# A four-layer graph network in one kernel: when the feature gathers of the first phase are issued, and where attention weights lie

## The chip, the cores and the metric

The kernel runs on one core of a Trainium2 chip. The metric is the device time of one execution in microseconds (us). TensorE (PE) multiplies matrices and transposes; VectorE (DVE) does comparisons, scans and elementwise work; ScalarE (ACT) applies functions and copies; GpSimd (POOL) issues the indirect DMAs, which gather or scatter rows by a list of indices; SyncE (SP) issues plain DMAs.

## What is computed

A graph has 100000 nodes with 16 features and 50000 edges sorted by their target node. Four residual layers follow each other, each on the layer-normed and rectified features: two graph attention (GAT) layers, two relational layers, a sum over edges with a rational message, and relational attention. The attention layer is cut here to what matters:

```
h = (x @ W).reshape(N, heads, outc)
e = leaky_relu(alpha_s[src] + alpha_d[dst], 0.2)
m = segment_max(e, dst);  p = exp(e - m[dst])
z = segment_sum(p, dst);  alpha = p / (z[dst] + 1e-16)
out = segment_sum(h[src] * alpha[:, :, None], dst) + b
```

Every node has a loop to itself besides. The first attention layer has 3 heads of 32 channels, the second one head of 32.

## The kernel before

The kernel is a sequence of phases. Each allocates its own buffers and semaphores and consists of one program for each engine; between two phases stands a barrier of all engines. Nodes lie 800 to a partition (C), edges 392 to a partition (T). A helper `hold(engine, sem, value)` (L50) makes an engine wait for a semaphore. Another, `paced` (L58), lets gather number s wait until the batch of eight gathers that lies two batches back has landed.

**Phase a** (64 to 1305 us) has three parts for the engines other than POOL. First comes a histogram of the edges by target: for each of NB = 56 batches of TB = 7 edge columns VectorE writes 14 one-hot tiles in fp16 (L514, L515), and TensorE adds up 14 products of them in two PSUM banks (L600) and raises `hist_ok` at the batch's end; VectorE waits for `hist_ok` of the batch two back. Then one chain of operations on VectorE turns counts into positions. The dense part follows: the node features are normed (L412 to L426), and in NSUB = 50 sub-steps TensorE transposes (L613), scores (L620), multiplies up to four half parts of the hidden layer in four banks (L632), ScalarE takes ReLU and Exp of each half part (L674, L676), VectorE combines them (L584) and raises `act_ok` once for each half part, so 200 times, and TensorE multiplies down (L643). SyncE stores the results. POOL meanwhile issues 392 gathers of input rows into `pay` (L497), one for each edge column, in one loop with `paced` (L496) in front of each. The rows in `pay` are first used in the next phase, c, which sorts the edges and scatters them to their places, four scatters a group.

**Phase g1** (2120 to 3041 us) is the first attention layer over edges. POOL gathers 336 columns of source rows (L1091). Edges are treated in nine chunks. For a chunk VectorE computes scores and arguments into `pr`, ScalarE takes their Exp in place (L1179), and VectorE multiplies the gathered rows by the weights (L1238), copies the weights (L1241) and runs 51 scans (L1244) that sum along the edges of a target. `pr` lies in SBUF. Then the sums are normalised and mixed, and 25 sub-steps like those of phase a follow: transposes (L1114), up products in the four banks from column 1024 (L1127), ScalarE (L1193, L1195), VectorE (L1340), down products (L1138) and rows (L1315). Before the four up products of a sub-step TensorE waits for `exp_ok` of the whole previous sub-step.

**Phase g2** (3041 to 3900 us) does the same for the second attention layer with one head: gathers into a ring (L1427) that POOL fills when `ring_free` says so, Exp in place in `pr` (L1537), product, copy and 33 scans a chunk (L1577 to L1581).

All phases after g2 are the same in both kernels.

Of the kernel before, what the change touches and what calls it, by code (L numbers as in the profile page):

```python
# [5 lines left out]
ALU = mybir.AluOpType  # L6
# [7 lines left out]
P = 128  # L14
# [60 lines left out]
def gnn_kernel(nc, x, src, dst, edge_attr_16, edge_type_8, edge_type_90, edge_weight,  # L75
# [45 lines left out]
    with ExitStack() as top:  # L121
# [43 lines left out]
        with ExitStack() as ctx:  # L165
# [3 lines left out]
            def sem(name):  # L169
                return semaphore(ctx, name)  # L170
# [269 lines left out]
        with ExitStack() as ctx:  # L440
# [10 lines left out]
            COLS = Q * FEAT  # L451
            SUB = 16
            NSUB = C // SUB
            PER = Q // SUB
            hi = tmp("hi", [P, 2, TB, 2, P], F16)
            lo = tmp("lo", [P, 2, TB, LO], F16)
# [33 lines left out]
            with nc.Block() as block:  # L490
                @block.gpsimd
                def _(pool):
                    nc.gpsimd.iota(home[:], pattern=[[1, C]], base=SLOTS, channel_multiplier=ROWS,
                                   allow_small_or_imprecise_dtypes=True).then_inc(home_ok, 1)
                    for s in range(T):
                        paced(pool, gat_in, s)  # L496
                        pool.indirect_dma_start(pay[:, s, 8:PAY], None, x,  # L497
                                                bass.IndirectOffsetOnAxis(gidx[:, s:s + 1], 0)
                                                ).then_inc(gat_in[s // BATCH], 16)
                    all_landed(pool, gat_in, 0, T)  # L500
# [533 lines left out]
        with ExitStack() as ctx:  # L1034
# [3 lines left out]
            def sem(name):  # L1038
# [25 lines left out]
            ps = psum_all(ctx, "ps_g1")  # L1064
            ps_o = ps[:, 3072:4096].rearrange("p (a z) -> p a z", z=512)[:, :, 0:8 * (CH + 2)].rearrange(
                "p a (n w) -> p a n w", w=CH + 2)
            gat_in = [sem(f"gat_in{n}") for n in range(T // BATCH)]
            out_s = [sem("out0"), sem("out1")]
            step_s, arg_ok, exp_e, mix_ok, tail_ok, bm_ok, reach_ok, at_ok, att_ok, ext_ok = (sem(n) for n in (
# [16 lines left out]
            with nc.Block() as block:  # L1086
# [18 lines left out]
                def _(pe):  # L1105
# [12 lines left out]
                    flip(0)  # L1118
                    for n in range(NCH):
                        hold(pe, copy_ok, n + 1)  # L1120
                        if n:
                            hold(pe, exp_ok, 4 * n)
                        for u in range(4):
                            to = ps[0:HID, 1024 + 512 * u:1536 + 512 * u]
                            for j in range(2):
                                at = 512 * (u % 2) + 256 * j
                                last = mm(to[:, 256 * j:256 * (j + 1)], w1_half[:, u // 2].rearrange("p h c -> p (h c)"),  # L1127
                                          mix_t[:, at:at + 256], start=True, stop=True)
                            last.then_inc(up_ok, 1)
# [32 lines left out]
                @block.scalar  # L1162
                def _(act):
                    def copy(n):
                        hold(act, flip_ok, n + 1)
                        nc.scalar.copy(mix_t[:], ps[0:HID, 0:8 * P]).then_inc(copy_ok, 1)

                    def edges(n):
                        for what, i in edge_at.get(n, []):
                            w = widths[i]  # L1170
                            if what == "extend":
                                hold(act, at_ok, 1)
                                nc.scalar.copy(reach_t[:].rearrange("p h q -> p (h q)"),
                                               ps[:, 512:512 + HEADS1 * P]).then_inc(att_ok, 1)
                                w += 1
                            if (what, i) in exps:
                                hold(act, arg_ok, exps[what, i])
                                if what == "score":
                                    last = nc.scalar.activation(pr[:, :, 0:w], pr[:, :, 0:w], ACT.Exp)  # L1179
                                elif what == "reach":  # L1180
                                    nc.scalar.activation(shrink[:], shrink[:], ACT.Exp)
                                    last = nc.scalar.activation(reach[:], reach[:], ACT.Exp)
                                else:
                                    last = nc.scalar.activation(ab[:, :, 0:w], ab[:, :, 0:w], ACT.Exp)
                                last.then_inc(exp_e, 1)

                    edges(-1)
                    copy(0)
                    for n in range(NCH):
                        for u in range(4):  # L1190
                            hold(act, up_ok, 4 * n + u + 1)
                            view = ps[0:HID, 1024 + 512 * u:1536 + 512 * u]
                            nc.scalar.activation(pos[:, u], view, ACT.Relu, bias=b1_col[:, 1:2],  # L1193
                                                 scale=1.0 / SELU_ALPHA)
                            nc.scalar.activation(ex[:, u], view, ACT.Exp, bias=b1_col[:, 0:1]).then_inc(exp_ok, 1)  # L1195
                        edges(n)
                        if n + 1 < NCH:
                            copy(n + 1)

                @block.vector  # L1200
                def _(dve):
# [33 lines left out]
                    def edge_sum(i):  # L1235
# [1 line left out]
                        hold(dve, exp_e, exps["score", i])  # L1237
                        v.tensor_tensor(S[:, 1:1 + w, 0:HF].rearrange("p q (h f) -> p q h f", f=FEAT),  # L1238
                                        bcast(ring1[:, c0:c0 + w, 0:FEAT].unsqueeze(2), [P, w, HEADS1, FEAT]),
                                        bcast(pr[:, 0, 0:w].unsqueeze(3), [P, w, HEADS1, FEAT]), ALU.mult)  # L1240
                        step.link(v.tensor_copy(S[:, 1:1 + w, Z0:M0], pr[:, 0, 0:w]))  # L1241
                        for j in range(M0):
                            h = j // FEAT if j < HF else j - HF
                            last = v.tensor_tensor_scan(S[:, 1:1 + w, j], pr[:, 1, 0:w, h], S[:, 1:1 + w, j],  # L1244
                                                        S[:, 0, j:j + 1], ALU.mult, ALU.add)
                        step.link(last)
                        step.link(v.copy_predicated(kept[:, 0:w],
# [114 lines left out]
        with ExitStack() as ctx:  # L1362
# [30 lines left out]
            row = tmp("row", [P, 2, QN, FEAT])  # L1393
            t = ln_buffers(ctx, QN, "g2", 1)[0]
            ps = psum_all(ctx, "ps_g2")
            gat_in = [sem(f"gat_in{n}") for n in range(T // BATCH)]
            hs_in, out_s = [sem("hs_in0"), sem("hs_in1")], [sem("out0"), sem("out1")]
            step_s, lead_ok, x_clear, arg_ok, exp_e, tail_ok, bm_ok, reach_ok, at_ok, att_ok, ext_ok = (
# [21 lines left out]
            with nc.Block() as block:  # L1420
# [68 lines left out]
                def _(act):  # L1489
# [22 lines left out]
                    for n in range(NCH):  # L1512
# [18 lines left out]
                        for what, i in edge_at.get(n, []):  # L1531
# [2 lines left out]
                            w = widths[i]  # L1534
                            hold(act, arg_ok, exps[what, i])
                            if what == "score":
                                last = nc.scalar.activation(pr[:, :, 0:w], pr[:, :, 0:w], ACT.Exp)  # L1537
                            else:
                                last = nc.scalar.activation(ab[:, :, 0:w], ab[:, :, 0:w], ACT.Exp)
                            last.then_inc(exp_e, 1)  # L1540
# [6 lines left out]
                def _(dve):  # L1547
# [25 lines left out]
                    def edge_sum(i):  # L1573
# [1 line left out]
                        hold(dve, exp_e, exps["score", i])  # L1575
                        r0 = QN * (i % NR)
                        v.tensor_tensor(S[:, 1:1 + w, 0:CH], ring[:, r0:r0 + w, 0:CH],  # L1577
                                        bcast(pr[:, 0, 0:w].unsqueeze(2), [P, w, CH]), ALU.mult).then_inc(ring_free, 1)
                        step.link(v.tensor_copy(S[:, 1:1 + w, Z0], pr[:, 0, 0:w]))
                        for j in range(M0):  # L1580
                            last = v.tensor_tensor_scan(S[:, 1:1 + w, j], pr[:, 1, 0:w], S[:, 1:1 + w, j],  # L1581
                                                        S[:, 0, j:j + 1], ALU.mult, ALU.add)
                        step.link(last)
                        step.link(v.copy_predicated(kept[:, 0:w],
# [1064 lines left out]
```

## Time and profile before

| | |
|---|---|
| median of the runs | 8605.08 us (8596.4 to 8612.05, 3 runs) |
| profiled execution | 8610.18 us, its span 8608.4 us |
| PE busy | 3087.1 us (36%), 13056 instructions |
| DVE busy | 3685.0 us (43%), 8866 instructions |
| ACT busy | 1171.1 us (14%) |
| POOL busy | 4256.0 us (49%), 3949 instructions |

No engine is busy for more than half of the span, and the phases have different limits. The page of the profile cuts the span into 40 slices of 215 us; its rows for the engines, in tenths, are these (the first six slices are phase a):

```profile
PE   1127889993114411451127711361111110111232
PEld 0014775552103311341126601351111110011121
DVE  3027448995016621673014412485432325422454
ACT  0002554441002201330001100010000000000000
POOL 5750005665770066506740075405888882577555
PEclk7558889996556655555556655575555555555666
```

The groups of instructions that the change touches, in the page's order, with busy time, mean duration of one, and the idle time in front of them with its releaser:

```profile
L497 POOL DMA_INDIRECT pay<-in_x,gidx x392 | 403.7, 1030 | 119.3 <-issue 117.8
L1091 POOL DMA_INDIRECT ring<-t_gat,src_i x336 | 351.6, 1046 | 145.6 <-issue 101.7
L600 PE MATMUL ps_a<-a_lo,a_hi 128*128 128x400 f16 x784 | 173.6, 384 | 508.6 <-issue 390.0
L514 DVE TENSOR_SCALAR a_hi<-iota_hi,h_f 128x256 f16<-128x256 f16 x392 | 113.6, 290 | 488.9 <-remote 376.4
```

### The profile page before, as it was taken

To read this page: it belongs to the slowest core of one execution; us is meant where nothing else is said; L and a number is where in the kernel's file an instruction comes from. 1 tells how busy PE (TensorE), PEld (TensorE's weight loads), DVE (VectorE), ACT (ScalarE), POOL (GpSimd) and SP (SyncE) were. 2 spreads that over 40 slices of the span, in tenths; PEclk is the share of its full clock that TensorE was granted. 3 is DMA by queue.
4 is the path that set the end of the run, shared out by engine and by line. 5 is a ranking of instruction groups with operands and counts; after the bars stand their busy time and mean duration, and the time that the engine had idled before them with its cause. 6 is when DMAs were issued, how large, how long until landed. Compare 5 with 4: busy or idle time off the path is not lost. (4 is left out here: it accounts for less than half of the span.)

```text
span 8608.4 us, 52587 instructions
## 1 busy us (share of the span) xinstructions
PE 3087.1 (36%) x13056; PEld 2333.1 (27%) x13056; DVE 3685.0 (43%) x8866; ACT 1171.1 (14%) x1912; POOL 4256.0 (49%) x3949
## 2 busy tenths in 40 slices
PE   1127889993114411451127711361111110111232
PEld 0014775552103311341126601351111110011121
DVE  3027448995016621673014412485432325422454
ACT  0002554441002201330001100010000000000000
POOL 5750005665770066506740075405888882577555
PEclk7558889996556655555556655575555555555666
DMA  2000112221110021211112211111222223311011
GB/s 34 6 5 16 53 51 71 66 66 34 11 9 13 13 57 25 61 56 20 14 34 92 89 25 23 45 60 53 47 41 29 39 20 93 98 19 18 29 41 51
DMA packets 283407, 350.60 MB, mean 41 GB/s; under 512 B 133518, under 2 KB 204432, under 8 KB 281970
## 3 DMA queue, kind: packets, MB, share of 16 engines
q1 hardware_dynamic: 112158, 295.24, 10.4%
q0 software_dynamic: 169376, 41.40, 6.5%
q10 hardware_dynamic: 1576, 10.60, 0.5%
q8 instruction: 112, 1.84, 0.1%
q14 instruction: 185, 1.52, 0.1%
HBM read 231.06 MB, written 122.29 MB: 41 GB/s over the span
## 5 line engine op out<-in xcount | busy, mean ns | idle before, releaser
L754 POOL DMA_INDIRECT t_sort<-pay,c_pos x392 | 406.2, 1036 | 988.4 <-DVE c_pos L820 876.5
L2068 POOL DMA_INDIRECT r_ring<-t_rel,idx x392 | 387.5, 989 | 753.0 <-POOLq L119 523.9
L1427 POOL DMA_INDIRECT g_ring<-t_gat,idx x392 | 404.0, 1031 | 645.4 <-POOLq L119 465.8
L2292 POOL DMA_INDIRECT acc<-l_rows,l_uniq x392 | 629.5, 1606 | 124.3 <-issue 118.6
L2278 POOL DMA_INDIRECT l_ring<-t_mix,idx x392 | 422.2, 1077 | 423.0 <-POOLq L119 303.8
L1757 POOL DMA_INDIRECT r_ring<-t_rel,idx x392 | 400.0, 1020 | 410.6 <-POOLq L119 287.8
L2556 PE MATMUL ps_l<-w_rel,l_pick 128*128 128x256 f32 x784 | 268.6, 517 | 845.5 <-DVE l_pick L2585 600.9
L2515 POOL DMA_INDIRECT l_ring<-t_last,idx x392 | 397.7, 1014 | 333.1 <-ACTq L2510 209.2
L846 PE MATMUL ps_c<-plane,c_hit 128*128 128x400 f32 x1568 | 544.1, 500 | 2.5 <-ACT c_hit L772 2.5
L2525 POOL DMA_INDIRECT fin<-X,home_i x393 | 389.8, 992 | 287.7 <-DVE X L2614 168.6
L2333 PE MATMUL ps_l<-l_msg,l_alike 128*128 128x16 f32 x784 | 174.8, 374 | 988.0 <-DVE l_msg L2398 909.7
L497 POOL DMA_INDIRECT pay<-in_x,gidx x392 | 403.7, 1030 | 119.3 <-issue 117.8
L2556 PEld LDWEIGHTS ps_l<-w_rel,l_pick 128*128 128x128 f32 x784 | 207.3, 271 | 906.4 <-issue 863.4
L2333 PEld LDWEIGHTS ps_l<-l_msg,l_alike 128*128 128x128 f32 x784 | 171.0, 331 | 991.8 <-issue 991.8
L1091 POOL DMA_INDIRECT ring<-t_gat,src_i x336 | 351.6, 1046 | 145.6 <-issue 101.7
L2602 DVE TENSOR_TENSOR l_wide<-ps_l,l_ring 128x2048 f32<-128x2048 f32 x49 | 112.3, 2292 | 646.2 <-DMA acc<-l_rows,l_uniq 642.2
L600 PE MATMUL ps_a<-a_lo,a_hi 128*128 128x400 f16 x784 | 173.6, 384 | 508.6 <-issue 390.0
L846 PEld LDWEIGHTS ps_c<-plane,c_hit 128*128 128x128 f32 x1568 | 296.6, 191 | 210.9 <-issue 4.4
L1988 DVE TENSOR_TENSOR r_row<-rb_row,r_ps 128x1280 f32<-128x1280 f32 x30 | 44.6, 1488 | 710.6 <-DMA pay<-in_x,gidx 441.2
L514 DVE TENSOR_SCALAR a_hi<-iota_hi,h_f 128x256 f16<-128x256 f16 x392 | 113.6, 290 | 488.9 <-remote 376.4
L1816 PE MATMUL r_ps<-rel_w,r_msg_t 128*128 128x32 f32 x784 | 177.0, 400 | 239.6 <-ACT r_msg_t L1887 128.8
L816 DVE SCALAR_TENSOR_TENSOR c_junk<-iota_lo,lo_f,ps_c 128x400 f32<-128x400 f16 x392 | 230.4, 624 | 51.9 <-PE ps_c L846 46.2
(528 smaller groups left out, 8355.9 us busy)
## 6 DMA issues: line engine op xcount, KB each, us to landing
c_rows_d<-row_dst SPq DMA_DIRECT2D x98, 256.0 KB
l_keys<-row_at SPq DMA_DIRECT2D x49, 512.0 KB
l_typs<-row_typ SPq DMA_DIRECT2D x49, 512.0 KB
g_hs<-t_gat SPq DMA_DIRECT2D x30, 660.0 KB
acc<-r_zero SPq DMA_DIRECT2D x60, 320.0 KB
t_rel<-r_row SPq DMA_DIRECT2D x30, 640.0 KB
r_hs<-t_rel SPq DMA_DIRECT2D x30, 640.0 KB
d_gain<-acc SPq DMA_DIRECT2D x30, 640.0 KB
```

What stands on the lines that cost most here:

```text
L497: pool.indirect_dma_start(pay[:, s, 8:PAY], None, x, bass.IndirectOffsetOnAxis(gidx[:, s:s + 1], 0)).then_inc(gat_in[s // BATCH], 16)
L754: pool.indirect_dma_start(t_sort, bass.IndirectOffsetOnAxis(pos[:, e:e + 1], 0), pay[:, e, :], None).then_inc(sent, 16)
L846: last = mm(ps[:, bank:bank + LO], hit[:, b, j, P * s:P * (s + 1)], plane[:, b, LO * j:LO * (j + 1)], start=(j == 0), stop=(j == 1))
L1091: pool.indirect_dma_start(ring1[:, s, :], None, t_gat1, bass.IndirectOffsetOnAxis(src_i[:, s:s + 1], 0)).then_inc(gat_in[s // BATCH], 16)
L1427: pool.indirect_dma_start(ring[:, s % (NR * QN), :], None, t_gat2, bass.IndirectOffsetOnAxis(idx2[:, s:s + 1], 0)).then_inc(gat_in[s // BA ...
L1757: pool.indirect_dma_start(ring[:, s % (NR * QN), :], None, table, bass.IndirectOffsetOnAxis(idx2[:, s:s + 1], 0)).then_inc(gat_in[s // BAT ...
L2068: pool.indirect_dma_start(ring[:, s % (NR * QN), :], None, t_rel2, bass.IndirectOffsetOnAxis(idx2[:, s:s + 1], 0)).then_inc(gat_in[s // BA ...
L2278: pool.indirect_dma_start(ring[:, s, :], None, t_mix, bass.IndirectOffsetOnAxis(idx2[:, s:s + 1], 0)).then_inc(gat_in[s // BATCH], 16)
L2292: pool.indirect_dma_start(acc[r], bass.IndirectOffsetOnAxis(uniq[:, s:s + 1], 0), rows[:, (s // ES) % RR, s % ES, :], None, compute_op=ALU.add
L2515: pool.indirect_dma_start(ring[:, s, :], None, t_last, bass.IndirectOffsetOnAxis(idx2[:, s:s + 1], 0)).then_inc(gat_in[s // BATCH], 16)
L2525: pool.indirect_dma_start(fin, bass.IndirectOffsetOnAxis(home_i[:, s:s + 1], 0), X[:, s, :], None).then_inc(sent[s // BATCH], 16)
L2556: last = mm(ps[:, at:at + 256], pick[:, e % 2, s], w_rel[:].rearrange("p i o -> p (i o)"), start=True, stop=True)
```

## The change

In phase a the wait on landed batches is taken away. The first 112 gathers are tied to the histogram: from the fourth on, two are issued for each batch that TensorE has finished. The gathers from the 117th on are tied to the dense part: four are issued for every two half parts that VectorE has finished. The last of these waits is for half part 138 of 200. The order of the dense products stays. In g1 and g2 the Exp writes the weights into PSUM (`pw`), and the product, the copy and the scans read them there. In g1 `pw` takes the bank at column 2560, so the up products rotate over three banks, with a wait on ScalarE before each half part; in g2 it lies at column 4000.

```diff
@@ phase a
+            BURST = 4
+            assert 2 * ((T - 1 - 2 * NB) // BURST) <= 4 * NSUB
                     for s in range(T):
-                        paced(pool, gat_in, s)
+                        rest = s - 2 * NB
+                        if rest < 0 and s % 2 == 0 and s >= 4:
+                            hold(pool, hist_ok, s // 2 - 1)
+                        elif rest >= BURST and rest % BURST == 0:
+                            hold(pool, act_ok, 2 * (rest // BURST))
                         pool.indirect_dma_start(pay[:, s, 8:PAY], None, x, ...
@@ phase g1
+            pw = ps[:, 2560:2560 + 2 * EW * HEADS1].rearrange("p (a q h) -> p a q h", a=2, h=HEADS1)
                         hold(pe, copy_ok, n + 1)
-                        if n:
-                            hold(pe, exp_ok, 4 * n)
                         for u in range(4):
-                            to = ps[0:HID, 1024 + 512 * u:1536 + 512 * u]
+                            if 4 * n + u >= 3:
+                                hold(pe, exp_ok, 4 * n + u - 2)
+                            bank = 1024 + 512 * ((4 * n + u) % 3)
+                            to = ps[0:HID, bank:bank + 512]
...
-                                    last = nc.scalar.activation(pr[:, :, 0:w], pr[:, :, 0:w], ACT.Exp)
+                                    last = nc.scalar.activation(pw[:, :, 0:w], pr[:, :, 0:w], ACT.Exp)
...
-                                        bcast(pr[:, 0, 0:w].unsqueeze(3), [P, w, HEADS1, FEAT]), ALU.mult)
-                        step.link(v.tensor_copy(S[:, 1:1 + w, Z0:M0], pr[:, 0, 0:w]))
+                                        bcast(pw[:, 0, 0:w].unsqueeze(3), [P, w, HEADS1, FEAT]), ALU.mult)
+                        step.link(v.tensor_copy(S[:, 1:1 + w, Z0:M0], pw[:, 0, 0:w]))
                         for j in range(M0):
                             h = j // FEAT if j < HF else j - HF
-                            last = v.tensor_tensor_scan(S[:, 1:1 + w, j], pr[:, 1, 0:w, h], S[:, 1:1 + w, j],
+                            last = v.tensor_tensor_scan(S[:, 1:1 + w, j], pw[:, 1, 0:w, h], S[:, 1:1 + w, j],
@@ phase g2
+            pw = ps[:, 4000:4000 + 2 * QN].rearrange("p (a q) -> p a q", q=QN)
```

In g2 the same four places (Exp, product, copy, scans) use `pw` in the same way.

## Rows read from the trace of the kernel before

**Rows 1.** Busy windows of phase a, by stretch; the first line names the columns.

```profile
core 0: us, PE busy (x) PEld busy (x) DVE busy (x) ACT busy (x) POOL busy (x), PEclk, DMA share, GB/s
64.00:90.00 26.00, 14.35 (x68) 7.16 (x69) 18.43 (x72) 0.00 (x0) 20.32 (x20) 1.00 0.23 56
90.00:588.00 498.00, 58.87 (x186) 24.55 (x184) 41.35 (x182) 0.00 (x0) 384.18 (x374) 0.55 0.08 6
...
614.00:734.00 120.00, 95.67 (x518) 48.75 (x518) 114.50 (x521) 0.00 (x0) 0.00 (x0) 0.97 0.00 1
734.00:766.00 32.00, 2.00 (x9) 1.60 (x10) 27.44 (x32) 1.93 (x3) 0.00 (x0) 0.51 0.00 0
766.00:1305.00 539.00, 466.89 (x2695) 389.03 (x2694) 253.21 (x331) 289.96 (x527) 0.00 (x0) 0.82 0.13 50
```

**Rows 2.** Waits, 100 to 600 us: engine, line, releaser: total us, times, longest.

```profile
PE ps_a L600 <- issue: 377.5, 11, 35.1
DVE a_hi L514 <- remote: 319.9, 9, 36.1
```

**Rows 3.** Timeline, phase a: start, duration, instruction, count, idle before with its releaser.

```profile
71.09 7.39 PE L600 MATMUL ps_a<-a_lo,a_hi 128*128 128x400 f16 x28 [22.43 <-DVE a_lo L515]
...
131.27 0.29 DVE L514 TENSOR_SCALAR a_hi<-iota_hi,h_f 128x256 f16<-128x256 f16 x1 [31.95 <-remote]
...
586.89 0.95 POOL L497 DMA_INDIRECT pay<-in_x,gidx  x1 [0.30 <-issue]
600.97 0.29 DVE L514 TENSOR_SCALAR a_hi<-iota_hi,h_f 128x256 f16<-128x256 f16 x1 [35.30 <-remote]
...
614.42 0.29 DVE L514 TENSOR_SCALAR a_hi<-iota_hi,h_f 128x256 f16<-128x256 f16 x1 [10.36 <-remote]
```

**Rows 4.** Timeline, 1395 to 1412 us, phase c: scatters in fours.

```profile
1398.41 0.97 POOL L754 DMA_INDIRECT t_sort<-pay,c_pos  x1 [1.66 <-DVE c_pos L820]
...
1404.56 5.54 PE L846 MATMUL ps_c<-plane,c_hit 128*128 128x400 f32 x16
...
1405.14 0.97 POOL L754 DMA_INDIRECT t_sort<-pay,c_pos  x1 [1.66 <-DVE c_pos L820]
```

**Rows 5.** Groups by line and form, 766 to 1305: busy, mean ns, idle.

```profile
L632 PE MATMUL ps_a<-a_norm_t,w_dense 128*96 128x256 f32 x800 | 245.7, 476 | 0.0
L643 PE MATMUL ps_a<-w_ext,a_act_t 96*128 96x34 f32 x1600 | 196.0, 276 | 7.5 <-DVE a_act_t L584 1.8
...
L584 DVE SCALAR_TENSOR_TENSOR a_act_t<-a_ex,a_pos 96x512 f32<-96x512 f32 x200 | 137.6, 688 | 240.1 <-ACT a_ex L676 240.0
...
L426 DVE SCALAR_TENSOR_TENSOR a_norm<-a_ln_cent,a_ln_small 128x1280 f32<-128x1280 f32 x9 | 13.4, 1494 | 0.3
```

**Rows 6.** Timeline, 900 to 930 us: two sub-steps of the dense part.

```profile
914.59 5.98 PE L632 MATMUL ps_a<-a_norm_t,w_dense 128*96 128x256 f32 x16
...
924.57 3.66 PE L632 MATMUL ps_a<-a_norm_t,w_dense 128*96 128x256 f32 x16
```

**Rows 7.** Timeline, 2129 to 2160 us, phase g1: first chunk beside gathers.

```profile
2129.56 2.56 DVE L1238 TENSOR_TENSOR g_S<-ring,g_pr 128x2304 f32<-128x2304 f32 x1 [1.93 <-ACT g_pr L1179]
2130.13 2.80 POOL L1091 DMA_INDIRECT ring<-t_gat,src_i  x1 [0.30 <-issue]
...
2132.30 11.08 DVE L1244 TENSOR_TENSOR_SCAN g_S<-g_pr,g_S 128x48 f32<-128x48 f32 x51
...
2138.99 5.21 POOL L1091 DMA_INDIRECT ring<-t_gat,src_i  x1 [0.30 <-issue]
```

**Rows 8.** Groups by line and form, 2120 to 3041 us: PSUM and SBUF sources.

```profile
L1340 DVE SCALAR_TENSOR_TENSOR g_act_t<-g_ex,g_pos 96x512 f32<-96x512 f32 x100 | 68.8, 688 | 271.2 <-ACT g_ex L1195 145.4 <-issue 125.8
...
L1315 DVE TENSOR_TENSOR g_row<-ps_g,w_const 128x528 f32<-128x528 f32 x25 | 17.4, 698 | 0.0
```

**Rows 9.** Busy windows of phase g1, same columns as Rows 1.

```profile
2177.00:2588.00 411.00, 48.47 (x163) 36.33 (x160) 44.37 (x99) 19.01 (x29) 304.60 (x303) 0.51 0.11 10
2603.00:3041.00 438.00, 219.37 (x1167) 180.28 (x1165) 280.91 (x706) 127.93 (x205) 0.00 (x0) 0.64 0.04 14
```

More of the change, by code:

```diff
@@ L1191, in _ @@
                             hold(act, up_ok, 4 * n + u + 1)
-                            view = ps[0:HID, 1024 + 512 * u:1536 + 512 * u]
+                            bank = 1024 + 512 * ((4 * n + u) % 3)
+                            view = ps[0:HID, bank:bank + 512]
                             nc.scalar.activation(pos[:, u], view, ACT.Relu, bias=b1_col[:, 1:2],
@@ L1536, in _ @@
                             if what == "score":
-                                last = nc.scalar.activation(pr[:, :, 0:w], pr[:, :, 0:w], ACT.Exp)
+                                last = nc.scalar.activation(pw[:, :, 0:w], pr[:, :, 0:w], ACT.Exp)
                             else:
@@ L1577, in edge_sum @@
                         v.tensor_tensor(S[:, 1:1 + w, 0:CH], ring[:, r0:r0 + w, 0:CH],
-                                        bcast(pr[:, 0, 0:w].unsqueeze(2), [P, w, CH]), ALU.mult).then_inc(ring_free, 1)
-                        step.link(v.tensor_copy(S[:, 1:1 + w, Z0], pr[:, 0, 0:w]))
+                                        bcast(pw[:, 0, 0:w].unsqueeze(2), [P, w, CH]), ALU.mult).then_inc(ring_free, 1)
+                        step.link(v.tensor_copy(S[:, 1:1 + w, Z0], pw[:, 0, 0:w]))
                         for j in range(M0):
-                            last = v.tensor_tensor_scan(S[:, 1:1 + w, j], pr[:, 1, 0:w], S[:, 1:1 + w, j],
+                            last = v.tensor_tensor_scan(S[:, 1:1 + w, j], pw[:, 1, 0:w], S[:, 1:1 + w, j],
                                                         S[:, 0, j:j + 1], ALU.mult, ALU.add)
```

## The prediction

> **What bounds the kernel now.** The phases stand behind barriers, so each phase's length counts in full, and a busy share over the whole span says little. I read the busy windows first, phase by phase, then the waits of the stretch that looked wrong, then its timeline.
>
> The windows show that phase a runs in three parts [rows 1]. From 90 to 588 us POOL gathers without rest (374 gathers), and in that time TensorE gets 186 matmuls done and VectorE 182 operations. From 614 to 734 us, with POOL silent, the same two engines do 518 and 521. One histogram batch is 14 matmuls and 14 comparisons, so the free pace is 518 / 14 = 37 batches in 120 us, or 3.2 us each with the edges of the window and 3.0 inside it, and the pace beside gathers is 13.3 batches in 498 us, or 37 us each. The data of the gathers (`pay`) is not needed by anyone in this phase.
>
> The waits say where the 37 us go: VectorE waits 319.9 us in nine pieces of up to 36.1 us in front of the first comparison of a batch, for something that the profile calls remote, and TensorE stands 377.5 us in eleven pieces [rows 2]. VectorE's only wait there is `hist_ok`, which TensorE raises with the last matmul of a batch. So TensorE's work, or its message, reaches the other engines some 31 to 35 us late. The timeline bears this out in three steps [rows 3]. At the start of the phase two batches run in 7.39 us although POOL already gathers every 1.25 us. From 131.27 us on a batch comes after 31.95 us of idleness. The last gather starts at 586.89 us, the late message still takes until 600.97, the next one comes 13.4 us later at 614.42, and from there the batches follow each other freely. The lateness is thus something that builds up while gathers follow each other without a break, and that drains within about 27 us once they stop. I can't see in this trace what it is that backs up; the sum only needs that it builds up.
>
> A second place shows what breaks do. In phase c POOL scatters four rows' worth, waits 1.66 us for positions, and scatters four again, one group per 1405.14 - 1398.41 = 6.73 us, while TensorE's matmuls take 5.54 us of each group [rows 4]. No hand-over is late there, in 98 groups. Phase g1 repeats the bad pattern: 303 gathers and only 163 matmuls in 411 us, then 1167 matmuls in 438 us [rows 9].
>
> **Part 1, histogram batches.** Two gathers per batch are 2 x 1.25 = 2.5 us of POOL in a batch of at least 3.0 us, so POOL rests at least 0.5 us in each. The bounds for a batch are 3.0 us, the free pace, and 26 / (68 / 14) = 5.4 us, the pace of the first 26 us with 20 gathers in them and the start-up counted in [rows 1]; the two batches in 7.39 us give 3.7. I take 3.5, near that last row. Then 56 x 3.5 = 196 us, from 67.8 to 264 us, where before the histogram ended at 734. The added wait stands on POOL with only gathers behind it, and nobody in this phase waits for those. The removed waits on landings (`paced`) cost nothing before: POOL's gap in front of a gather is 0.30 us with them [rows 3]. Next comes the chain that turns counts into positions, 32 us on VectorE [rows 1], unchanged: POOL has only six gathers to issue in it. It ends at 296.
>
> **Part 2, dense product.** Without gathers a sub-step takes 539 / 50 = 10.8 us on average [rows 1], and 10.0 us between the two matmul groups 914.59 and 924.57 [rows 6]. Now 69 bursts of four gathers are spread over it, two bursts a sub-step, so 34.5 sub-steps carry gathers and 15.5 do not. POOL needs 8 x 1.25 = 10.0 us in such a sub-step. Some gathers get longer beside VectorE. The nearest rows are in g1: while VectorE runs an operation with two SBUF sources (2.56 us) and 51 scans (11.08 us), five gathers take 2.80, 1.05, 2.78, 1.01 and 5.21 us instead of 0.95 each (first and longest in [rows 7]), 8.1 us lost in 13.9 us of such work, or 0.6 us per us. In the dense part such work is 4 x 0.69 us a sub-step for the activation, and three lines like L426 with 9 x 1.49 us each in 50 sub-steps, 0.8 us [rows 5]: 0.6 x (2.75 + 0.8) = 2.1 us. With 0.4 us for two hand-overs, a round figure of mine without a row, POOL comes to 12.5 us, over the 10.8 us of the others. POOL becomes the slower party by a little. But it isn't needed by the others: it only matters through the lateness, and it can't run ahead, because every burst waits for `act_ok` of two half parts. So the pace should settle where POOL has just enough rest. I take 12.5 us, with 10.8 (all hidden) as the lower end and 20.8 as the upper (10.8 plus two bursts of 5.0 us in which TensorE does nothing). The sum is 34.5 x 12.5 + 15.5 x 10.8 = 431 + 167 = 598 us, 59 more than before. Phase a ends at 296 + 598 = 894 us instead of 1305: **411 us less**. What covers the gathers is the dense work itself; if that cover were gone (the upper end), 34.5 x 8.3 = 286 us would come back.
>
> **Part 3, g1.** The weights move from SBUF to PSUM. VectorE's own time hardly changes: an operation over 528 elements from PSUM takes 698 ns and one over 512 from SBUF 688 [rows 8]. The copy of the weights is nine small operations, too little to matter. The scans I bound between no change and 5% of 8 chunks x 11.08 us, 4.4 us. The gathers beside them should no longer grow, which gives POOL up to 8.1 us in each of the two chunks that lie beside gathers, 16 us in all; nothing if one source in SBUF is enough to block. POOL's end sets that of the starved stretch, at 2588. Against it: POOL without these pauses may bring the lateness on earlier, and one sub-step that falls into it is worth 438 / (1167 / 56) = 21 us more. Three instead of four banks for the up products: a product now waits for ScalarE's second half part before it instead of for the whole previous sub-step. ScalarE is 128 us busy in 438 [rows 9], so it holds nobody for long; 0 to 5 us. Behind the waiting product stand the next sub-step's transposes and the down products, and VectorE waits for these. Together -16 to +26; I take -3.
>
> *The Trainium skill on this.* Gathers grow to 2.80 and 5.21 us beside VectorE operations with two SBUF sources [rows 7]. The Trainium skill, "SBUF — State Buffer", section "Who interferes with whom", says that such an operation contends with a GpSimd instruction that reads SBUF, while descriptor generation, inferred there to need only the write side, is spared by `tensor_tensor`. By the first half part 3 gains up to 16 us, by the second nothing; the trace shows gathers held by exactly such operations, so it speaks for the first. The same section says that PE and ACT never wait on anyone.
>
> **Part 4, g2.** The same move for 33 scans a chunk. The gathers there wait for ring slots, so time that POOL saves is mostly waited away: 0, within 10 us either way.
>
> **Sum.** The profiled execution is 8610.2 us, 8608.4 us of it span and 1.8 around it; the median of the runs is 8605.1, 5 less. 8610 - 411 - 3 - 5 = 8191, so **8190 us**. A measurement can tell about 0.2% here, 17 us.
>
> **Rivals.** *All hidden.* Batches at 3.2 us and sub-steps at 10.8: phase a ends at 68 + 179 + 32 + 539 = 818, 487 less, so 8115 us. For it: the two batches in 7.39 us beside gathers, and phase c. Against: POOL's 12.5 us of work in 10.8.
>
> *Lateness stays in the dense part.* POOL rests much less there than in phase c (0.4 us after four gathers at best, against 1.66). If TensorE does next to nothing during a burst, as between 90 and 588 us (186 matmuls for 374 gathers, two for a burst of four), sub-steps take 20.8 us: 34.5 x 20.8 + 167 = 885 us, phase a ends at 1181, and the kernel takes 8610 - 124 - 8 = 8478 us. For it: the first long lateness, from 99.3 to 131.3 us [rows 3], set in after only some 27 gathers (20 up to 90 us [rows 1], and one every 1.25 us from there). Against: the waits limit POOL to what TensorE has finished, so that a backlog can't grow past a burst.
>
> *Slower: every burst costs a drain.* If the lateness comes with any few gathers and each burst has to drain as the last did, 600.97 - 586.89 = 14.1 us, then POOL waits for TensorE and TensorE for the drain: a sub-step takes 10.8 + 2 x (5.0 + 14.1) = 49 us, and phase a ends at 296 + 34.5 x 49 + 167 = 2153 us, 848 later: 9450 us. It turns to the slower side once a sub-step with gathers passes (1305 - 296 - 167) / 34.5 = 24.4 us. Against it: phase c.
>
> *Pacing does nothing.* If something else than gathers held TensorE until 614 us, the histogram would end near 734 again and the kernel at about 8600 us. The sentence of the skill above that TensorE waits on nobody would point there. Against it: the free pace begins 27 us behind the last gather [rows 3], and in g1 too right behind the stretch with the gathers [rows 9].
>
> **How the numbers follow.** Forecast with its own range of 8130 to 8330 (a batch of 4.5 us and a sub-step of 15 at the upper end, 56 + 86 us more): 0.62. All hidden: 0.12. Lateness stays in the dense part: 0.17. Every burst costs a drain: 0.05. Pacing does nothing: 0.04. The range takes in the first three, 8100 to 8490, and leaves 0.1 or a little more out. Faster by over 17 us 0.91, within it 0.04, slower 0.05.
>
> **What the profile would show.** Right: in phase a no idle time of VectorE over 5 us in front of L514; the last histogram matmul near 264 us; in the dense part gathers in fours, POOL idle for `act_ok` in front of each, 12 to 13 us a sub-step up to about 725 us and 10.8 after it; in g1's first chunk gathers of about 1 us beside L1244, and the pattern of 163 matmuls for 303 gathers unchanged. Wrong: `remote` waits of 10 us and more in the histogram (then the drain rival), dense sub-steps near 20 us with single matmuls 1 to 3 us apart while a burst runs (then the third), or an unchanged 734 us. The weakest step is the 12.5 us, since no row shows bursts of four with so little rest.

## The result and the profile after

The changed kernel takes 8199.2 us (median of 4 runs, 8194.2 to 8212.5), the kernel before in the same session 8600.7; the ratio is 0.9534, with an interval of 0.9517 to 0.955. The profiled execution has a span of 8200.5 us. The forecast was 8190. But the sum comes out by terms that miss in opposite directions, so part of the nearness is luck, and part of the experiments ran on other chips, on which the same kernel before takes 6610 us and the effect that the whole prediction is about does not show. Both are told below.

Busy windows of the changed kernel, with the columns of [rows 1]:

```profile
core 0: us, PE busy (x) PEld busy (x) DVE busy (x) ACT busy (x) POOL busy (x), PEclk, DMA share, GB/s
90.00:256.00 166.00, 131.05 (x705) 66.54 (x704) 149.49 (x692) 0.00 (x0) 129.48 (x101) 0.96 0.06 6
256.00:291.00 35.00, 1.80 (x9) 1.01 (x7) 30.41 (x35) 1.93 (x3) 4.48 (x4) 0.56 0.02 1
291.00:775.00 484.00, 382.08 (x1888) 307.50 (x1887) 183.39 (x237) 205.63 (x372) 284.59 (x276) 0.72 0.17 45
775.00:933.00 158.00, 140.52 (x812) 117.25 (x812) 70.42 (x94) 84.40 (x155) 0.52 (x1) 0.82 0.13 49
1803.00:2204.00 401.00, 60.43 (x230) 48.50 (x230) 54.25 (x106) 25.02 (x38) 298.00 (x292) 0.51 0.10 10
2220.00:2640.00 420.00, 205.14 (x1137) 168.81 (x1137) 274.77 (x698) 121.57 (x197) 0.00 (x0) 0.65 0.04 13
```

Below the line with the names, the first row stands against 498 us of [rows 1] with 186 matmuls: the histogram now gets 705 matmuls done in 166 us, with two gathers in each batch. The second is the chain. The third and fourth together are the dense part. The fifth is g1 beside its gathers, and 292 gathers leave it 230 matmuls, the pattern of [rows 9] (303 and 163). The sixth is g1 behind its gathers. In front of the first comparison of a batch VectorE's waits for what the profile calls remote have shrunk from 376.4 us to one of 8.1:

```profile
L520 DVE TENSOR_SCALAR a_hi<-iota_hi,h_f x392: 267/275/480, 67.9 to 253.3; 128x256 f16<-128x256 f16 x196
...
  remote: 8.1, 1
```

Phase by phase, from the first gather or scatter of one phase to that of the next (us):

| | before | after | difference | forecast |
|---|---|---|---|---|
| a | 1259.5 | 886.3 | -373 | -411 |
| c and k | 795.5 | 794.3 | -1 | 0 |
| g1 | 921.5 | 906.0 | -15.5 | -3 |
| g2 | 871.5 | 872.1 | +0.6 | 0 |
| all later phases, to the last scatter | 4669.7 | 4650.3 | -19.4 | 0 |

### The profile page after: what moved, and what is told of

The parts are those of the page before. It is cut to its first block and busy times, and to the rows that moved or that the text cites. A ratio compares the mean times of both kernels' runs of the same rounds, so it can differ in the third digit from the quotient of the medians.

```text
span 8200.5 us, 52407 instructions
## 1 busy us (share of the span) xinstructions
PE 3084.1 (38%) x13056; PEld 2341.1 (29%) x13056; DVE 3678.2 (45%) x8866; ACT 1170.1 (14%) x1912; POOL 4265.6 (52%) x3949
## 5 line engine op out<-in xcount | busy, mean ns | idle before, releaser
L503 POOL DMA_INDIRECT pay<-in_x,gidx x392 | 433.8, 1107 | 276.8 <-DVE a_act_t L590 151.6
L638 PE MATMUL ps_a<-a_norm_t,w_dense 128*96 128x256 f32 x800 | 267.4, 496 | 16.3 <-issue 14.7
L590 DVE SCALAR_TENSOR_TENSOR a_act_t<-a_ex,a_pos 96x512 f32<-96x512 f32 x200 | 138.1, 690 | 245.0 <-ACT a_ex L682 215.5
```

The source lines that it names most:

```text
L503: pool.indirect_dma_start(pay[:, s, 8:PAY], None, x, bass.IndirectOffsetOnAxis(gidx[:, s:s + 1], 0)).then_inc(gat_in[s // BATCH], 16)
```

## Where the dense part lost what the forecast gave it

The forecast for phase a was 411 us less and it became 373. The histogram ended at 256 us, one batch in 3.37 us (forecast: 3.5), and the chain at 291 (296). The dense part then took 642 us and not 598. Up to the last gather (median 947 ns, last start 774.6 us) a sub-step takes (775 - 291) / 34.5 = 14.0 us, where I had 12.5; after it (933 - 775) / 15.5 = 10.2, where I had 10.8.

```profile
L503 POOL DMA_INDIRECT pay<-in_x,gidx x392: 942/947/2087, 65.1 to 774.6; - x196
```

The waits from 291 to 775 us show why 14.0:

```profile
POOL pay L503 <- DVE a_act_t L590: 151.6, 22, 37.6
...
ACT a_row L666 <- remote: 91.3, 8, 15.1
DVE a_row L579 <- remote: 89.0, 9, 14.6
```

POOL is not the slower party, as my sum had it: it stands 151.6 us waiting for `act_ok`. TensorE's results come late again, in 17 pieces of up to 15.1 us at the row copies and the scores. So it is the rival "lateness stays in the dense part" in a mild form: some bursts build lateness up, the wait on `act_ok` stops POOL, it drains, and the next ones run freely.

Single sub-steps show it too, taken from the first L590 of one to that of the next (L584 in the kernel before). No sub-step settles at 12.5 or 14.0 us. In the kernel before, 27 of the first 34 take 8.2 to 10.1 us and seven, about one in five, 18 to 19. In the changed kernel 14 take 17 to 22 us, six take 11 to 12 and the others 8.2 to 10.5; together the 34 take 472 us and not 373. The working of 0.6 us of blocked POOL time per us of VectorE work does not hold: the 276 gathers of this stretch keep POOL busy for 284.6 us, 1.03 each, so eight of them with their gaps of 0.30 take 10.7 us, and POOL could have kept up. That the sum was only 1.5 us off is luck.

## In g1 two things happened at once

Timeline of g1's beginning, in the changed kernel and then, in one row, in the kernel before:

```profile
1757.97 8.70 DVE L1253 TENSOR_TENSOR_SCAN g_S<-ps_g,g_S 128x48 f32<-128x48 f32 x41
...
1774.76 0.32 DVE L1253 TENSOR_TENSOR_SCAN g_S<-ps_g,g_S 128x48 f32<-128x48 f32 x1 [1.07 <-issue]
...
1776.16 0.32 DVE L1253 TENSOR_TENSOR_SCAN g_S<-ps_g,g_S 128x48 f32<-128x48 f32 x1 [1.08 <-issue]
...
1787.39 3.16 DVE L1256 COPY_PREDICATED g_kept<-head_mask,g_S 128x2592 f32<-128x2592 uint32 x1 [9.52 <-DMA pay<-in_x,gidx]
...
1810.56 1.92 PE L1121 MATMUL ps_g<-ident,g_mix 128*96 128x128 f32 x8 [69.98 <-issue]
```

```profile
2158.64 1.92 PE L1114 MATMUL ps_g<-ident,g_mix 128*96 128x128 f32 x8 [43.70 <-DVE g_mix L1303]
```

Gathers now pass beside the 51 scans at 0.95 us each, as forecast, and nothing like the 5.21 us of [rows 7] is left there. But after 41 scans in 8.70 us the other ten follow singly or in pairs, 1.4 us apart. Some 17 unbroken gathers are enough to make VectorE's own instructions slow, not only TensorE's messages. The first transposes come 1810.56 - 1745.7 = 64.9 us after the first gather of the phase; before it was 2158.64 - 2120.0 = 38.6 us. (In the later run of the same kernel, called whole below, 32 scans pass before they slow down, and the transposes come after 52.9 us.) Against this stands POOL's gain: its gathers start over 444.3 us instead of 454.6, 10.3 us less where I had up to 16, and the rest of the phase behind the last gather's start is another 5.2 us shorter. Together that is the 15.5 us.

The 19 us in phases that the change does not touch are in part plain variation. In the four profiled executions of kernels with the change on chips of this kind, whose code behind g2 is the same, the later phases take 4650.3, 4659.0, 4654.5 and 4659.8 us; the one trace of the kernel before has 4669.7. So they vary by 9.5 us among themselves, and the other 9.9 us between the nearest of them and the kernel before are one pair of executions and stay unexplained. Half of the 19 lies in the phase that scatters sums into `acc`, 1386.9 and 1377.8 us, which takes 1382.9 to 1387.6 in the other three.

## Experiments

**One chip is not like another.** The first four kernels ran on a chip on which the kernel before takes 6614 us (13 runs, 6601 to 6619). Phase a's part alone:

```diff
-                        paced(pool, gat_in, s)
+                        if rest < 0 and s % 2 == 0 and s >= 4:
+                            hold(pool, hist_ok, s // 2 - 1)
+                        elif rest >= BURST and rest % BURST == 0:
+                            hold(pool, act_ok, 2 * (rest // BURST))
```

> Only the phase a part of the change. If the gain is that of the broken-up gathers, phase a ends about 373 us earlier as in the changed kernel (951 instead of 1324 us to the first scatter) and the kernel takes 8225 to 8240 us, 0.957 of the kernel before; g1 keeps its 921 us. Rival: the 19 us that the phases after g2 lost come from the g1 and g2 edits or from moved code; then they are absent here, and the phases after g2 last as long as before to 2 us.

It took 6609.4 us, ratio 0.9997 (0.9988 to 1.0007): no difference. Its first scatter is at 837 us, and a_only's g1 lasts 655 us. The expectation was for a chip with 8600 us and can't be held against this number. Next, the changed kernel with all of phase a's gathers put behind the dense part (the first one waits for `act_ok` 200, and nothing else is changed):

> All gathers of phase a wait until the dense part is done. This gives the floor of the other work: 3.0 us a batch (histogram over by 240 us) and 10.8 us a sub-step (dense part 539 us, over by about 815 us) if gathers are what slows both; the gathers then take some 490 us by themselves and the phase ends near 1305 us, the kernel near 8600 us. Rival: part of the slowness is in the engines' own hand-overs; then batches take 3.3 us and sub-steps 12 us even without gathers.

It took 7038.5 us in its one run, since the gathers are then alone in their time (813 to 1301 us). Busy windows of phase a, first with gathers beside the work (a_only), then without (gathers_last):

```profile
90.00:240.00 150.00, 124.67 (x692) 63.91 (x691) 149.21 (x689) 0.00 (x0) 121.04 (x96) 1.00 0.07 6
300.00:600.00 300.00, 256.27 (x1471) 213.01 (x1472) 144.82 (x189) 160.71 (x292) 219.31 (x217) 0.81 0.22 57
```

```profile
90.00:240.00 150.00, 126.10 (x700) 64.67 (x697) 147.16 (x685) 0.00 (x0) 0.00 (x0) 1.00 0.00 1
300.00:600.00 300.00, 258.12 (x1476) 215.32 (x1477) 142.06 (x187) 161.70 (x295) 0.00 (x0) 0.81 0.14 53
```

From 300 to 600 us 217 gathers beside the dense part cost five matmuls of 1476. In the histogram it is 692 against 700. The free paces (150 / (700 / 14) = 3.0 us a batch, 300 / (1476 / 54) = 11.0 a sub-step) are those of the engines, and gathers cost next to nothing here. Nor does an unbroken row of them, as the same windows of g_only show, whose phase a is that of the kernel before:

```profile
90.00:240.00 150.00, 123.62 (x687) 63.38 (x685) 149.99 (x686) 0.00 (x0) 118.01 (x106) 1.00 0.07 7
300.00:600.00 300.00, 256.81 (x1486) 214.06 (x1486) 146.28 (x191) 162.59 (x296) 230.11 (x227) 0.81 0.23 59
```

The kernel before on the first kind gets 186 matmuls done in 498 us beside such a row [rows 1].

Only the weights in PSUM and the three banks (g_only):

> Only the weights in PSUM and the three banks. From the two traces: g1 about 15 us shorter, g2 the same, so 0.998 (8585 to 8595 us). In g1's first chunk the 51 scans should be starved by gathers that follow each other freely, and the first transposes come about 26 us later than before, as in the changed kernel. Rival: that delay belongs to phase a's change (the DMA state that it leaves); then it is absent here.

It took 6536.6 us, 0.9885 (0.9868 to 0.9901), 78 us less and five times the gain that I expected, and for a plain reason. Here eight of g1's nine chunks run beside gathers, not two. The gathers of g1, first with the weights in SBUF (a_only), then in PSUM (g_only), with minimum, median and maximum duration and first and last start:

```profile
L1097 POOL DMA_INDIRECT ring<-t_gat,src_i x336: 938/944/9549, 1599.7 to 2141.1; - x168
```

```profile
L1092 POOL DMA_INDIRECT ring<-t_gat,src_i x336: 940/944/3633, 1594.4 to 2070.5; - x168
```

They start over 541.4 and 476.1 us: 65 us for eight chunks, which is the 8.1 us a chunk of the forecast. The gathers' own durations account for all of it (440.2 us in sum and 374.9), so the third bank given up cost POOL nothing; the two edits were not run apart. The whole phase goes from 655 to 588 us. The scans are not starved there, and the transposes come 38.3 us after the first gather:

```profile
1606.72 10.74 DVE L1247 TENSOR_TENSOR_SCAN g_S<-ps_g,g_S 128x48 f32<-128x48 f32 x51
...
1632.71 1.92 PE L1115 MATMUL ps_g<-ident,g_mix 128*96 128x128 f32 x8 [43.39 <-DVE g_mix L1306]
```

So the late transposes of the changed kernel are no effect of the PSUM weights by themselves; they are seen only on the first kind of chip, when gathers come without a break.

**Is it the unbroken row?** In the changed kernel, only the histogram's gathers paced:

```diff
                             hold(pool, hist_ok, s // 2 - 1)
-                        elif rest >= BURST and rest % BURST == 0:
-                            hold(pool, act_ok, 2 * (rest // BURST))
```

> The histogram's gathers are paced, the 280 others follow each other without a wait from the end of the histogram on. If lateness builds up with any unbroken row of gathers, the dense part gets about 0.5 matmuls done per gather (some 140, under three sub-steps) until about 640 us and runs free from there: phase a ends near 1160 us and the kernel takes about 8440 us. Rival: the dense part stands the gathers better than the histogram did, since its matmuls are few and long; then phase a ends near 930 us and the kernel takes about 8200 us.

On the 6614 us chip, in one run: 6533.6 us, and the dense part at its free pace beside 228 gathers:

```profile
300.00:600.00 300.00, 256.82 (x1474) 214.69 (x1475) 142.91 (x188) 161.83 (x294) 230.78 (x228) 0.81 0.23 59
```

The next kernels ran on a chip of the first kind (kernel before 8574.6 us, 7 runs). The changed kernel again (whole):

> The changed kernel again, beside a new run of the kernel before. The last four kernels ran on a chip on which the kernel before takes 6614 us and not 8600, the gathers following each other as densely as ever: there the lateness does not occur, phase a's part was worth nothing (0.9997) and the PSUM part 0.9885. If lateness is a property of the chip, a chip with 8600 us for the kernel before gives 0.953 again, and one with 6614 us gives the product, 0.988 (6535 us). Rival: the first measurement's gain came from elsewhere and a chip with 8600 us gives another ratio.

8207.0 us, 0.9585 (0.9547 to 0.9623). With it, on the same chip:

> The kernel with only the histogram's gathers paced and 280 gathers in an unbroken row beside the dense part, again. On a chip with the kernel before at 6614 us: 6534 us as before. On one with 8600 us: if any unbroken row makes the others late, under three sub-steps done by 640 us, phase a over near 1160 us and the kernel at about 8440 us; if the dense part stands the gathers, phase a over near 950 us and the kernel at about 8200 us.

8423.3 us in one run, expected 8440. In its windows the dense part gets 108 matmuls done in 300 us beside 210 gathers, then 148 in the 30 us after them:

```profile
350.00:650.00 300.00, 37.09 (x108) 24.94 (x108) 15.98 (x19) 14.04 (x23) 210.12 (x210) 0.50 0.07 8
650.00:680.00 30.00, 27.23 (x148) 23.83 (x149) 10.18 (x15) 15.66 (x31) 0.00 (x0) 0.72 0.18 67
680.00:1100.00 420.00, 359.95 (x2086) 299.80 (x2085) 204.94 (x266) 227.83 (x414) 0.00 (x0) 0.81 0.14 52
```

This is the same code in the same stretch of its program as in the fence before, on two chips: 1474 matmuls and 108. On this second chip breaking the row is worth 8423 - 8207 = 216 us in the dense part alone, and the two kernels differ in nothing else. This also splits phase a's gain: the first scatter is at 1324 us in the kernel before (its trace is of the earlier session), at 1167 without the ties of the dense part, at 941 with them. So the histogram's ties bring 157 us net, since the gathers that they put off then hold up the dense part, and the dense ties another 226.

The whole change was not run on the faster kind; hist_only, which lacks only the ties of the dense part, gives 6533.6 / 6614.6 = 0.988 there, which is the PSUM part's gain. Set beside the 8199 us on the first kind, this leaves 1665 us between the chips after the change: g2 takes 872 us on the one and 627 on the other, the first relational phase 1043 and 616.

**Does it carry over to g1?** The changed kernel with g1's gathers tied to the half parts as well:

```diff
-                        paced(pool, gat_in, s, EARLY)
+                        chunk, j = s // EW, s % EW
+                        if j < 8:
+                            if j % 2 == 0:
+                                hold(pool, act_ok, 12 * chunk - 16 + j // 2)
+                        elif j < 28:
+                            if j == 8 and chunk > 1:
+                                hold(pool, act_ok, 12 * chunk - 12)
+                        elif (j - 28) % 3 == 0:
+                            hold(pool, act_ok, 12 * chunk - 11 + (j - 28) // 3)
```

> The changed kernel, with g1's gathers tied to the work too: two for each half part, 20 at once while VectorE has its long chain and TensorE nothing to do, then three for each half part. Where gathers make the other engines late (the kernel before at 8600 us), g1 should go from 906 us to about 670, since 25 sub-steps of 21 us at the free pace stretch to some 24, so 0.926 of the kernel before, 7960 us. Where they don't (6614 us) g1 can only lose: gathers are then bound to the slower party; 589 us become 620 or so, 0.993. Rival: the 48 gathers of a chunk fill the 63 us of three sub-steps so densely that lateness builds up in spite of the waits; then g1 stays above 850 us on the first kind of chip.

8034.4 us, 0.9385 (0.934 to 0.9429), 173 us under the changed kernel on the same chip, and the best version on such a chip. g1 lasts 743 us, not the 670 that I expected. The windows and waits say what is left, the waits for 1810 to 2400 us; the last row is g_only's on the faster chip, 1640 to 2180 us:

```profile
1810.00:2100.00 290.00, 116.61 (x573) 95.13 (x573) 133.56 (x317) 61.65 (x97) 159.94 (x156) 0.60 0.09 15
2100.00:2510.00 410.00, 160.34 (x772) 129.98 (x771) 209.39 (x503) 86.69 (x134) 166.50 (x168) 0.58 0.14 30
```

```profile
PE ps_g L1129 <- DVE g_mix L1320: 232.0, 6, 42.3
...
POOL ring L1106 <- DVE g_act_t L1357: 182.5, 34, 23.5
...
DVE g_S L1261 <- issue: 28.3, 49, 1.1
```

```profile
PE ps_g L1115 <- DVE g_mix L1306: 197.5, 8, 27.6
```

TensorE gets 573 matmuls done in 290 us instead of 230 in 401. But it still waits up to 42.3 us for the chunk's long chain on VectorE, 232.0 / 6 = 38.7 on average. Most of that is the chain itself, since on the faster chip it is 197.5 / 8 = 24.7 us; the other 14 us a chunk I put down to lateness. VectorE stands 49 times inside its scans, 28.3 us in all. That points to the 20 gathers that I let go at once during that chain, as already too many in a row, but fewer were not tried. Nor were these ties run on the faster kind, where I expected them to lose.

**Is it the rate or the row?** The kernel before with one small POOL operation in front of each gather of phase a:

```diff
+        def space(step):
+            step.link(nc.gpsimd.iota(pad[:], pattern=[[1, 128]], base=0, channel_multiplier=0,
+                                     allow_small_or_imprecise_dtypes=True))
...
                         paced(pool, gat_in, s)
+                        space(pad_step)
```

and the changed kernel with the same in k, g1, g2, the relational phases and the last one, with 128 or 320 columns. (The runs with _b repeat the others.)

> The kernel before, with one small POOL operation (an iota of 128 columns, some 0.2 to 0.4 us with its wait) in front of each of phase a's gathers, and no tie to the work: an unbroken row, but at about 1.65 us a gather and not 1.25. On a chip on which the kernel before takes 8600 us: if what counts is the rate at which gathers come, the histogram runs at 3.0 to 3.5 us a batch and is over by 270 us, and the dense part runs at 11 to 14 us a sub-step beside the rest; phase a is over near 950 us, the kernel at about 8210. Rival: any row without a real break builds lateness up, only more slowly; then batches take over 10 us after 100 us or so, and phase a is over later than 1200 us. On a chip with 6614 us: the same to 0.5%.

> The changed kernel, with the same small POOL operation in front of the gathers and scatters of the small sort phase, g1, g2, both relational phases and the last phase. On a chip with 8600 us for the kernel before: if the rate decides, these phases, which take 906, 872, 1040, 920 and 1220 us in the changed kernel, go to what 392 gathers at 1.65 us or their own work need, some 640, 690, 720, 690 and 1150 us: 7100 us, 0.83 of the kernel before. Rival: rate does not matter, only ties to the work do; then about 8200 us or more. On a chip with 6614 us: gathers last longer, 6600 to 6800 us.

> The same with 320 columns, some 0.2 us more a gather. If 1.65 us a gather is already slow enough, this one is slower than the one with 128 columns, by up to 0.2 us x 392 in each of five phases, 390 us at most; if 1.65 us is still too dense, it is faster. On a chip with 6614 us it is slower, by up to 390 us.

> The kernel before with one small POOL operation in front of each gather of phase a, again. On a chip with 6614 us for the kernel before it took 6622 us, nothing lost. On a chip with 8600 us: if the rate of the gathers decides, the histogram is over by 270 us, phase a near 950 us, the kernel at about 8210. Rival: an unbroken row still builds the lateness up; then phase a is over later than 1200 us and the kernel takes over 8450 us.

> The changed kernel with the same small operation in the later gather phases, again. On a chip with 6614 us for the kernel before it took 7148 us (1.081), since there the phases wait for gathers that are now slower. On a chip with 8600 us: if the rate decides, nothing is late any more and the kernel takes what it took on the other chip, some 7150 to 7250 us, 0.84; in the rival case 8200 us or more.

All of them ran on a chip with the kernel before at 6608 to 6609 us, so they could not answer the question: 6622.5 and 6637.1 us for phase a alone, 7147.5 (1.081, 1.0795 to 1.0831) and 7147.7 us for the later phases with 128 columns, and 7500.3 with 320. What they show is the price of such spacing where nothing is late. In the later phases it is 7147.5 - 6533.6 = 614 us against hist_only on the other chip of this kind, far over the 6600 to 6800 us that I expected for such a chip. POOL's cadence in the histogram is 1.5 us instead of 1.25, not the 1.65 that I expected, and the comparisons on VectorE get slower beside the iotas: it is busy all the time in both, and TensorE gets 600 matmuls in 150 us and not the 687 of g_only:

```profile
150.81 0.26 POOL L132 IOTA pad<- 128x128 f32 x1
...
151.35 0.96 POOL L506 DMA_INDIRECT pay<-in_x,gidx  x1 [0.27 <-POOL pad L132]
...
152.32 0.26 POOL L132 IOTA pad<- 128x128 f32 x1
...
152.85 0.96 POOL L506 DMA_INDIRECT pay<-in_x,gidx  x1 [0.27 <-POOL pad L132]
```

```profile
90.00:240.00 150.00, 108.03 (x600) 55.40 (x598) 150.00 (x600) 0.00 (x0) 121.69 (x200) 1.00 0.07 6
```

## Why the prediction was right, and where it was not

1. *The gathers hold the histogram.* Right in the session of the result and again in a later one on such a chip (702 matmuls in the same 166 us): 37 us a batch became 3.37. The sign that I named, no `remote` wait over 5 us, was too strict: there is one of 8.1 us. The rival "pacing does nothing" is what happens on the other chips (0.9997). The Trainium skill, "SBUF — State Buffer", section "Who interferes with whom", says that PE and ACT never wait on anyone, in a section on ports to SBUF. The faster chips agree with it, 1474 matmuls in 300 us beside 228 gathers. On the first kind it is 108, but no row shows that these matmuls wait for a port, so they don't refute it either.
2. *A sub-step of 12.5 us.* Wrong in its mechanism, and 1.5 us off in its number by luck. I built it from POOL's own time, 12.5 us, and let the pace settle where POOL has just enough rest. POOL's own time was 10.7 us, it waited 151.6 us for `act_ok`, and what set the pace was lateness that builds up in some bursts, in pieces of up to 15.1 us. 14.0 instead of 12.5 is 52 us. The sub-steps without gathers took 10.2 us and not 10.8, 9 us back; the histogram and the chain ended 5 us early. Against that rival the forecast held that the waits keep a backlog from growing past a burst; they limit the lateness (14.0 us and not 20.8) but don't prevent it. The 0.4 us for two hand-overs is a term that no run shows.
3. *g1 at -3.* It was -15.5, at the good end of my -16 to +26 (which leaves out the 4.4 us for scans that I had just bounded; with them it ends at +30). The gain of POOL was right in size where all chunks count (8.1 us a chunk, 65 us for eight chunks), and 10.3 us instead of 16 here. The risk that I named for TensorE, to be starved sooner, came true for VectorE: the transposes came 26 us later, and yet the phase did not get longer, since POOL's end sets that of the starved stretch, as the forecast had it.
4. *Nothing in the later phases.* The profiled pair differs by 19.4 us there, more than the 17 us that I took for what can be told, and no run ties it to the change. It brought 8199 nearer to 8190: the phases that the change touches gained 373.2 + 15.5 - 0.6 = 388 us, and the forecast had 414. From the 8605 us of before that alone would be 8217.

What stays open: what it is that backs up. The traces give one hint. On the first kind of chip the page names no landing for most transfers, on the other it does, as for this load in the kernel before and then in a_only:

```profile
c_rows_d<-row_dst SPq DMA_DIRECT2D x98, 256.0 KB
```

```profile
c_rows_d<-row_dst SPq DMA_DIRECT2D x98, 256.0 KB, 3.3
```

On the first kind most of the landing events of gathers are missing from the trace while gathers follow each other closely. Each gather raises its semaphore by 16. From 90 to 240 us the trace of the kernel before holds 226 such events beside 119 gathers, that of the changed kernel 1151 beside 90, and that of g_only on the faster chip 1667 beside 105. That fits an overload of the path on which completions are told, gathers' and engines' alike, but no run here isolated it, and the record does not tell whether the recording of these events itself takes part. Why chips differ is not known either. Each session ran on one chip, and only one chip is known to have been used twice (both times at 6609 us), so a state of the moment can't be told from a property of the chip. Whether a steady row at 1.5 us a gather would do on such a chip is also open.

## What to carry to other kernels

When another engine's work slows down beside a row of indirect DMAs whose results nobody needs yet, tie the DMAs to that work's progress by a semaphore, a few per step. In phase a this cost nothing where the effect was absent (0.9997); where it was present the changed kernel gained 4 to 5%, and 6% with g1's gathers tied as well (the weights in PSUM are in both figures). Check a long single-queue row of DMAs against the matmul count of the same window, not against busy shares. And before a gain of several per cent is booked, run the kernel on a second chip: here the same code differs by 30% from one to another.

## What the runs showed of the hardware that was not expected

- The kernel before takes 8527 to 8612 us in all runs of two sessions and 6599 to 6619 us in all runs of three others, on two other chips. The gathers' median duration is the same, 0.95 us (947 and 944 ns).
- On the slower kind, some 17 to 27 gathers in a row at 1.25 us make TensorE's messages up to 36 us late and VectorE's scans come 1.4 us apart instead of 0.21.
- Bursts of two in 3.37 us (1.69 us a gather) cause next to none of it, one wait of 8.1 us, and two of 12.2 together in the later run; bursts of four at 1.75 us a gather cause some.
- Scans whose weights lie in PSUM leave the gathers beside them at 0.95 us; with both sources in SBUF single gathers take up to 9.5 us. The Trainium skill, "SBUF — State Buffer", section "Who interferes with whom", says that a VectorE operation with two SBUF inputs contends with a GpSimd instruction that reads SBUF; the trace agrees, for the gathers at hand (5.21 us in [rows 7], 0.95 beside the same scans with PSUM weights).
